# Edge softmax of a graph layer: whole-tile sums repaired at their first and last node, and x loads issued at its outset

## The reference

```python
w = exp(scores - smax[dst])                     # smax: largest score of the node's edges, per head
alpha = w / maximum(segment_sum(w, dst)[dst], 1e-9)
pooled[:, h] = segment_sum(alpha[:, h:h+1] * p, dst)
mean_p = segment_sum(p, dst) / maximum(deg, 1)
gate = softmax(mean_p @ Wg.T + bg)              # over the 4 heads
out = x + sigmoid(sum over h of gate[:, h] * pooled[:, h])
```

## Time and profile before

| what | us |
|---|---|
| median of 3 runs | 880.24 (876.46 to 882.37) |
| profiled execution, its own time | 881.09 |
| its span, first to last instruction | 879.3 |
| DVE busy in the span | 528.9 |
| PE busy in the span | 558.0 |
| HBM read and written | 111.39 MB and 59.59 MB |

### The profile page before, as it was taken

One profiled execution on the slowest core, in us unless ns is written; L12 is line 12 of the kernel. 1 busy time (PEld: TensorE's weight loads), 2 busy tenths in 40 slices (PEclk: granted clock), 3 DMA queues, 4 the chain that ended last, 5 costly groups with the idle time before them and its releaser, 6 DMA issues.

```text
span 879.3 us, 12486 instructions
## 1 busy us (share of the span) xinstructions
PE 558.0 (63%) x2436; PEld 425.6 (48%) x2437; DVE 528.9 (60%) x1878; ACT 378.0 (43%) x645; POOL 437.8 (50%) x334
## 2 busy tenths in 40 slices
PE   4104211117999999688950006988887888877885
PEld 3002101105877776566730005867776666656664
DVE  3621010015999999777988895756665555555553
ACT  0011000004777776455720020445665666576564
POOL 5777777730000004565200000557777778787887
PEclk9655555556999999999985556999999999999998
DMA  6334434311333434877600004999999999999998
GB/s 177 103 106 127 130 104 129 105 50 53 117 111 106 120 98 125 261 242 240 224 27 0 0 0 148 302 386 322 305 323 339 311 304 336 336 333 327 339 333 299
DMA packets 135059, 171.41 MB, mean 195 GB/s; under 512 B 8110, under 2 KB 121604, under 8 KB 135022
## 3 DMA queue, kind: packets, MB, share of 16 engines
q10 hardware_dynamic: 90496, 89.83, 31.3%
q1 hardware_dynamic: 31678, 42.99, 15.7%
q0 software_dynamic: 12848, 38.20, 13.9%
HBM read 111.39 MB, written 59.59 MB: 194 GB/s over the span
## 4 chain that ended last, share of the span: by engine, by line
PE 40%; another core or an unknown queue 19%; DVE 12%; issue 11%; ACT 7%; POOL 4%; ACTq 3%; DVEq 2%; DMA 2%; POOLq 0%
PE bank L555 19%; PE bank L613 14%; PE bank L545 6%; ACT arena L429 4%; POOL arena L327 3%; DVE spread L913 3%; ACT bank L402 2%; DMA arena<-in_x_dram 2%; DVE arena L867 2%; ACTq L432 1%; DVEq L917 1%; DVE arena L827 1%; DVE arena L822 1%; DVEq L913 1%
## 5 line engine op out<-in xcount | busy, mean ns | idle before, releaser
L327 POOL TENSOR_TENSOR arena<-arena 128x1024 f32<-128x1024 f32 x96 | 224.8, 2350 | 185.7 <-ACT arena L429 184.8
L613 PE MATMUL bank<-p_keep,spread 128*128 x1172 | 278.0, 392 | 57.9 <-DVE spread L913 47.8
L555 PE MATMUL bank<-w_all,arena 128*128 128x264 f32 (+1 forms) x784 | 226.7, 415 | 104.4 <-issue 81.3
L913 DVE TENSOR_SCALAR spread<-bank,rel,wgt 128x128 f32<-128x128 f32 x586 | 195.8, 404 | 136.5 <-PE bank L613 84.8
L613 PEld LDWEIGHTS bank<-p_keep,spread 128*128 128x128 f32 x1172 | 222.0, 194 | 113.7 <-issue 84.8
L555 PEld LDWEIGHTS bank<-w_all,arena 128*128 128x128 f32 (+1 forms) x784 | 143.5, 204 | 127.2 <-issue 86.3
L314 POOL DMA_INDIRECT arena<-in_x_dram,idx x72 | 69.3, 962 | 190.8 <-ACT arena L366 170.2
L429 ACT ACTIVATE arena<-bank 128x1024 f32<-128x1024 f32 x97 | 99.2, 1022 | 150.2 <-PE bank L613 133.7
L374 ACT ACTIVATE arena<-bank 128x256 f32<-128x256 f32 x196 | 72.6, 371 | 169.6 <-remote 108.6
L314 POOL DMA_INDIRECT p_keep<-in_x_dram,idx x124 | 118.4, 955 | 43.0 <-issue 37.5
L545 PE MATMUL bank<-ident,arena 128*128 128x128 f32 x392 | 83.5, 297 | 62.3 <-remote 46.7
(11 more groups left out here) (161 smaller groups left out, 184.5 us busy)
## 6 DMA issues: line engine op xcount, KB each, us to landing
out_dram<-arena ACTq DMA_DIRECT2D x97, 512.0 KB, 4.4
arena<-in_x_dram ACTq DMA_DIRECT2D x73, 512.0 KB, 5.3
arena<-in_edge_attr_dram SPq DMA_DIRECT2D x48, 512.0 KB
arena<-in_x_dram POOLq DMA_DIRECT2D x24, 512.0 KB, 5.7
p_spill<-p_keep SPq DMA_DIRECT2D x16, 512.0 KB
p_keep<-p_spill SPq DMA_DIRECT2D x16, 512.0 KB, 5.3
p_keep<-in_x_dram,idx POOLq DMA_INDIRECT x124
arena<-in_x_dram,idx POOLq DMA_INDIRECT x72
```

The source lines that it names most:

```text
L327: pool.tensor_tensor(yout[:, slot, :, :], yout[:, slot, :, :], xin[:, slot, :, :], ALU.add).then_inc(summed, 1)
L555: last = nc.tensor.matmul(bank[0:n, 2 + t % 4, 0:NT], msg_t[:, t % 4, c, 0:n], w_all[:, c, :], start=(c == 0), stop=(c == KD - 1))
L613: nc.tensor.matmul(places[:, bass.ds(place, T)], spread[:, k0 + k, :], p_rows[:, bass.ds(p_at, T)], start=False, stop=True, skip_group_che ...
L913: v.tensor_scalar(spread[:, k, :], bank[:, 7, P:2 * P], rel[:, bass.ds(s0 + k, 1)], wgt[:, bass.ds(s0 + k, 1)], ALU.is_equal, ALU.mult).th ...
```

## The change

In the softmax each tile's own maxima serve its exponentials, and its own sums serve all its edges. The first and the last node of every tile, which may go on elsewhere, get their own small computation on 128 x 2 x 2 values per row (`own`, `far`, `mine`, `gain`, `ex`, `mn`), and the edges of these two nodes get their `c` by two predicated copies at the end. The eight rows are read from PSUM by the scans directly. Whether a node goes on is read from `next_f`, which five loads of single elements fill in the prologue; the bias of the gate is added to the matmul's bias there. The x loads of the first four groups are issued after the last normalization. `c` is ordered in two parts, 128 columns first, and DVE's first turn of the pooling is written out so that the rest is copied after it.

The diff, with the declarations of tiles left out:

```diff
 @block.sync
-sp.wait_ge(pads_set, 2)
+sp.wait_ge(pads_set, 3)
...
+    ends_of = dst[0:(TILES - 1) * P].rearrange("(t e) -> t e", e=P)
+    sp.dma_start(next_i[1:P, 0, 0:1], ends_of[0:P - 1, P - 1:P]).then_inc(next_in, 16)
+    sp.dma_start(next_i[0:TILES - P, 1, 0:1], ends_of[P - 1:TILES - 1, P - 1:P]).then_inc(next_in, 16)
+    sp.dma_start(next_i[0:P, 0, 1:2], ends_of[1:P + 1, 0:1]).then_inc(next_in, 16)
+    sp.dma_start(next_i[0:TILES - 2 - P, 1, 1:2], ends_of[P + 1:TILES - 1, 0:1]).then_inc(next_in, 16)
+    last_tile = (TILES - 1) * P
+    sp.dma_start(next_i[TILES - 2 - P:TILES - 1 - P, 1, 1:2],
+                 dst[last_tile:last_tile + 1].rearrange("(t e) -> t e", e=1)).then_inc(next_in, 16)
...
+pool.memset(next_i[:, :, :], -1).then_inc(pads_set, 1)
...
+act.wait_ge(ln_done, TILES)
+for g in range(XS):
+    load_x(g, g)
+
+act.wait_ge(keep_turned, 1)
+turned_keep = bank[0:C, 5, :].rearrange("p (s t) -> p s t", s=2)
+nc.scalar.activation(keep_row, turned_keep, ACT.Copy).then_inc(keep_set, 1)
+nc.scalar.activation(keep_neg, turned_keep, ACT.Copy, scale=BIG, bias=-BIG).then_inc(keep_set, 1)
+
 act.wait_ge(diff_ready, 1)
-nc.scalar.activation(val[:, 0:H, :], val[:, 0:H, :], ACT.Exp).then_inc(exp_done, 1)
-
+nc.scalar.activation(w_run, w_run, ACT.Exp).then_inc(exp_done, 1)
 act.wait_ge(diff_ready, 2)
-nc.scalar.activation(run[:, H:K, :], run[:, H:K, :], ACT.Exp).then_inc(exp_done, 1)
-
-
+nc.scalar.activation(ex, ex, ACT.Exp).then_inc(exp_done, 1)
+act.wait_ge(diff_ready, 3)
+nc.scalar.activation(run[:, 0:H, :], run[:, 0:H, :], ACT.Exp).then_inc(exp_done, 1)
+act.wait_ge(diff_ready, 4)
+nc.scalar.activation(mn, mn, ACT.Exp).then_inc(exp_done, 1)
...
+act.wait_ge(rows_read, 1)
...
-for g in range(XS):
-    load_x(g, g)
...
+pe.wait_ge(keep_ready, 1)
+turn_ends(lambda b, side: keep_cols[:, b, side, :], C, 5).then_inc(keep_turned, 1)
+pe.wait_ge(ends_ready, 1)
+turn_ends(lambda b, side: top[:, :, edge_of(b, side)], H, 6).then_inc(ends_turned, 1)
+turn_chain(H, 1)
+pe.wait_ge(ends_ready, 2)
+turn_ends(lambda b, side: own[:, b, side, :], C, 6).then_inc(ends_turned, 1)
+turn_chain(C, 2)
 pe.wait_ge(c_ready, 1)
-by_step(lambda b: flag[:, 2, b * P:(b + 1) * P], sel_1, 6, wgt_summed)
+c_of = lambda b: run[:, 8, b * P:(b + 1) * P]
+for n, o, cols in ((7, 2 * P, slice(0, P)), (6, 0, slice(P, STEPS))):
+    for b in range(BLK):
+        last = nc.tensor.matmul(bank[:, n, o:o + cols.stop - cols.start], c_of(b), sel_1[:, b, cols],
+                                start=(b == 0), stop=(b == BLK - 1))
+    last.then_inc(wgt_summed, 1)
...
+then(v.tensor_copy(bias[:, T:NT], bank[:, 4, KD * K:(KD + 1) * K]))
+then(v.tensor_tensor(bias[:, T + H:NT], bias[:, T + H:NT], bg_b[:, :], ALU.add))
+dve.wait_ge(next_in, 80)
+v.tensor_copy(next_f[:, :, :], next_i[:, :, :])
...
+v.memset(joins[:, 0:RW + 1:P], 0.0)
+then(v.tensor_tensor(per_blk(same)[:, :, 1:P], dst_f[:, :, 1:P], dst_f[:, :, 0:P - 1], ALU.is_equal))
+v.memset(tot[:, 0, :], 1.0)
+v.tensor_scalar(neg, joins, 1.0, BIG, ALU.subtract, ALU.mult)
+v.tensor_tensor(cm, next_f[:, :, :], dst_f[:, :, 0:P:P - 1], ALU.is_equal)
+then(v.tensor_tensor(one_node, dst_f[:, :, 0], dst_f[:, :, P - 1], ALU.is_equal))
+then(v.tensor_tensor(wc, cm, for_b(one_node), ALU.mult))
+v.tensor_copy(keep_cols, for_k(wc, C)).then_inc(keep_ready, 1)
+dve.wait_ge(rows_turned, 1)
+for n in range(H):
+    ins = v.tensor_tensor_scan(w_run[:, n, :], neg_same, row(n), 0.0, ALU.add, ALU.max)
+then(ins)
+dve.wait_ge(rows_turned, 2)
+for n in range(H):
+    ins = v.tensor_tensor_scan(top[:, n, ::-1], neg_next[:, ::-1], w_run[:, n, ::-1], -BIG,
+                               ALU.add, ALU.max)
+then(ins)
+dve.sem_inc(ends_ready, 1)
+v.tensor_tensor(w_run, bank[:, 0:2, :].rearrange("p b (k e) -> p (b k) e", k=2), top, ALU.subtract
+                ).then_inc(diff_ready, 1)
+for n in range(H, K):
+    v.tensor_tensor_scan(run[:, n, :], same, row(n), 0.0, ALU.mult, ALU.add)
+v.tensor_tensor_scan(run[:, K, :], same, tot[:, 0, :], 0.0, ALU.mult, ALU.add).then_inc(rows_read, 1)
+v.tensor_scalar(cneg, cm, 1.0, BIG, ALU.subtract, ALU.mult)
+v.tensor_scalar(wneg, one_node, 1.0, BIG, ALU.subtract, ALU.mult)
 v.tensor_scalar(end, same_next, -1.0, 1.0, ALU.mult, ALU.add)
+def link(k, keeps, pad, ops, count):
+    dve.wait_ge(ends_turned, count)
+    ends = bank[0:k, 6, :].rearrange("p (s t) -> p s t", s=2)
+    v.memset(chain_pads, pad)
+    v.tensor_tensor_scan(chain[0:k, 0, 1:TP + 1], keeps[0:k, 0, :], ends[:, 1, :], pad, *ops)
+    then(v.tensor_tensor_scan(chain[0:k, 1, 0:TP][:, ::-1], keeps[0:k, 1, ::-1], ends[:, 0, ::-1], pad, *ops))
+    dve.sem_inc(chain_ready, 1)
+from_far = bank[:, 7, 2 * P:2 * P + BLK * 2 * C].rearrange("p (b s k) -> p b s k", b=BLK, s=2)
+dve.wait_ge(keep_set, 2)
+link(H, keep_neg, -BIG, (ALU.add, ALU.max), 1)
+dve.wait_ge(exp_done, 1)
+for n in range(H):
+    ins = v.tensor_tensor_scan(run[:, n, :], same, w_run[:, n, :], 0.0, ALU.mult, ALU.add)
+then(ins)
+then(v.tensor_tensor(run, run, end.unsqueeze(1).broadcast_to([P, C, RW]), ALU.mult))
+dve.wait_ge(chain_turned, 1)
+own_top = at_ends(top, H)
+then(v.tensor_tensor(far_m, from_far[:, :, :, 0:H], for_k(cneg, H), ALU.add))
+v.tensor_tensor(m_all, own_top, far_m, ALU.max)
+then(v.tensor_tensor(ex, swap(far_m), for_k(for_b(wneg), H), ALU.add))
+then(v.tensor_tensor(m_all, m_all, ex, ALU.max))
+v.tensor_tensor(ex, own_top, m_all, ALU.subtract).then_inc(diff_ready, 1)
+for n in range(C):
+    ins = v.tensor_tensor_scan(tot[:, n, ::-1], same_next[:, ::-1], run[:, n, ::-1], 0.0,
+                               ALU.mult, ALU.add)
+then(ins)
+dve.wait_ge(exp_done, 2)
+own_tot = at_ends(tot, C)
+v.tensor_tensor(own[:, :, :, 0:H], own_tot[:, :, :, 0:H], ex, ALU.mult)
+then(v.tensor_copy(own[:, :, :, H:C], own_tot[:, :, :, H:C]))
+dve.sem_inc(ends_ready, 1)
+over_h = lambda a: a.unsqueeze(1).broadcast_to([P, H, RW])
+deg = run[:, 8, :]
+then(v.tensor_scalar(deg, tot[:, K, :], 1.0, None, ALU.max))
+then(v.reciprocal(deg, deg))
+then(v.tensor_tensor(run[:, 0:H, :], tot[:, H:K, :], over_h(deg), ALU.mult))
+link(C, keep_row, 0.0, (ALU.mult, ALU.add), 2)
+then(v.tensor_tensor(run[:, 4:6, :], run[:, 0:2, :], run[:, 2:4, :], ALU.max))
+then(v.tensor_tensor(run[:, 4, :], run[:, 4, :], run[:, 5, :], ALU.max))
+v.tensor_tensor(run[:, 0:H, :], run[:, 0:H, :], over_h(run[:, 4, :]), ALU.subtract).then_inc(diff_ready, 1)
+dve.wait_ge(chain_turned, 2)
+flat3 = lambda a: a.rearrange("p b s k -> p (b s) k")
+flat2 = lambda a: a.rearrange("p b s -> p (b s)")
+mine = own
+then(v.tensor_tensor(far, from_far, for_k(cm, C), ALU.mult))
+v.tensor_tensor(mine, mine, far, ALU.add)
+then(v.tensor_tensor(far_w, swap(far), for_k(for_b(one_node), C), ALU.mult))
+then(v.tensor_tensor(mine, mine, far_w, ALU.add))
+then(v.tensor_scalar(dg, mine[:, :, :, K], 1.0, None, ALU.max))
+then(v.reciprocal(flat2(dg), flat2(dg)))
+then(v.tensor_tensor(mn, mine[:, :, :, H:K], for_k(dg, H), ALU.mult))
+then(v.tensor_reduce(flat2(mx), flat3(mn), AX.X, ALU.max))
+v.tensor_tensor(mn, mn, for_k(mx, H), ALU.subtract).then_inc(diff_ready, 1)
+sums, total = tot[:, 0:H, :], run[:, 8, :]
+pair = lambda a: a.rearrange("p (g k) e -> p g k e", g=2)
+then(v.tensor_scalar(sums, sums, 1e-9, None, ALU.max))
+then(v.tensor_tensor(tot[:, 4:6, :], pair(sums)[:, :, 0, :], pair(sums)[:, :, 1, :], ALU.mult))
+v.tensor_tensor(tot[:, 6, :], tot[:, 4, :], tot[:, 5, :], ALU.mult)
 for b in range(BLK):
+    v.tensor_scalar(sel_1[:, b, :], step_tile[:, :], tile_f[:, b:b + 1], None, ALU.is_equal)
+dve.wait_ge(exp_done, 3)
+eg = run[:, 0:H, :]
+v.tensor_tensor(run[:, 4:8, :], w_run, eg, ALU.mult)
+then(v.tensor_tensor(tot[:, 7:9, :], run[:, 0:2, :], run[:, 2:4, :], ALU.add))
+v.tensor_tensor(tot[:, 7, :], tot[:, 7, :], tot[:, 8, :], ALU.add)
+then(v.tensor_tensor(pair(run[:, 4:8, :]), pair(run[:, 4:8, :]), pair(sums)[:, :, ::-1, :], ALU.mult))
+dve.wait_ge(exp_done, 4)
+then(v.tensor_reduce(flat2(se), flat3(mn), AX.X, ALU.add))
+then(v.tensor_scalar(far[:, :, :, 0:H], mine[:, :, :, 0:H], 1e-9, None, ALU.max))
+then(v.tensor_tensor(far_m, far[:, :, :, 0:H], for_k(se, H), ALU.mult))
+v.reciprocal(far_m.rearrange("p b s k -> p (b s k)"), far_m.rearrange("p b s k -> p (b s k)"))
+then(v.tensor_tensor(m_all, mn, ex, ALU.mult))
+v.tensor_tensor(gain, m_all, far_m, ALU.mult)
+then(v.tensor_tensor(tot[:, 6, :], tot[:, 6, :], tot[:, 7, :], ALU.mult))
+v.reciprocal(tot[:, 6, :], tot[:, 6, :])
+then(v.tensor_tensor(run[:, 0:2, :], pair(run[:, 4:8, :])[:, :, 0, :], pair(run[:, 4:8, :])[:, :, 1, :], ALU.add))
+then(v.tensor_tensor(run[:, 2:4, :], run[:, 0:2, :], tot[:, 5:3:-1, :], ALU.mult))
+v.tensor_tensor(total, run[:, 2, :], run[:, 3, :], ALU.add)
+by_end = lambda b, side: run[:, 4 + side, b * P:(b + 1) * P]
+for h in range(H):
+    for b in range(BLK):
+        for side in range(2):
+            w_of, g_of = w_run[:, h, b * P:(b + 1) * P], gain[:, b, side, h:h + 1]
+            if h == 0:
```

(67 more changed lines are left out.)

166 lines of the change are left out of this document (42 added, 124 removed).

## The result

The changed kernel takes 844.41 us (median, 843.76 to 848.87), the kernel before 878.35 us (876.19 to 882.37) in runs beside it: a ratio of 0.9619, 95% interval 0.9567 to 0.9671, 33.9 us less. Forecast were 850.0 us and 30.2 us less. The profiled execution took 844.58 us, with a span of 842.8. All ratios here leave out the executions in which the chip was in a slower state; the medians do not.

The account below looks back on a forecast made before the run. DVE was taken to bound the softmax, and bytes most of the pooling. From the profiled 881.09 us, - 28.5 - 2.0 + 0.3 = 850.9, or 850.0 against the median 880.24; range 842 to 857.

Parts of the forecast that it names:

- DVE bounds the softmax, and what it is spared comes off in full: Softmax start to `c_ready`, 81.4 us: DVE is busy for 74.2, so whatever it is spared the whole kernel is spared.
- The new sequence, 52.9 us: Softmax on DVE, priced instruction by instruction up to `c_ready`: 52.9 us against 81.4, a gain of 28.5 us.
- Nothing late in the hand-offs' place: Softmax: work between each question and its answer removes 5 us of DVE waiting; a failed cover would cost about 1 us.
- From `c_ready` to the first step, 6.3 us: Ordering before the pooling: 6.3 us instead of 8.3, a gain of 2.0 us, bounds 0.8 and 3.5.
- The x loads are worth nothing: Four loads of 512 KB moved from the pooling's start into the softmax: none credited, bounds 0 and 6.3 us.
- The prologue, 0.3 us: Five single-element loads ahead of the weights on SP, plus POOL's memset, cost 0.3 us in all, bounds 0 and 1.5.
- The x loads (1): Rival, chance 0.12: the moved x loads' 6.3 us come off the pooling's saturated stretch, giving 843.7 us.
- a dear sequence (3): Rival, chance 0.12: softmax small operations at 0.3 us each, dear predicated copies and one cover gone add 7.3 us: 857.
- The clock (2): Rival, chance 0.10: at the pooling's start TensorE's clock returns sooner, saving 2.0 us, giving 848.0.
- (4): Rival, chance 0.02: slower, since PE's clock stays at 0.50 at the pooling's start; 75 us of it would give 884.
- (5): Rival, chance 0.02: the main loop lands elsewhere, a few slow tiles more or less, 3 to 5 us either way.
- The prediction's last sign of being wrong: Pooling, first matmul to the end: the forecast is wrong if it takes 334 or 346 us, not 340 as now.

Follow-up runs that it names:

- The test without the merge: Kernel before without the merge of the carries into every edge (52 SCALAR_TENSOR_TENSORs and two masks): 692.26 us against 705.39, ratio 0.981.
- The kernel with one copy: Changed kernel, but DVE waits for both parts of the ordering before it copies `wgt`: 848.42 us, ratio 0.9716 to the kernel before.
- the last four runs: Changed kernel 677.04 us; with single-element loads behind the weights 668.08; that plus 32 PE transposes 671.58; kernel before with those loads ahead of the weights 712.38.

## Why the prediction was right, point by point

**DVE bounds the softmax, and what it is spared comes off in full: right.** The test without the merge gave 14.8 us for 14.7 in the stretch. In the whole time it gave 13.1 us, with an interval of 10 to 17, so that some of it could be lost behind.

**The new sequence, 52.9 us: measured 50.3.** The dear terms were sized well: scans 17.9 for 18.3, the 1024s 6.0 for 6.2, the twelve SCALAR_TENSOR_TENSORs 3.5 for 3.5, the two predicated copies 0.46 each for 0.45. What was too dear was the small change: 31 small operations took 4.6 us for 5.6, since many have no wait behind them, and the next instruction starts some 0.1 us after them; and the hand-offs 0.14 where they occur at all, some 0.6 for 1.2. The scans that read PSUM took 0.60 us each, like the others, so reading PSUM directly was free and the four copies were saved. The Trainium skill, "VectorE: DVE Perf Modes", section "Rules for kernel authors", says to copy PSUM to SBUF first where many operations follow; for these scans the trace shows nothing that the copy would have gained.

**Nothing late in the hand-offs' place: right.** DVE has no wait above 0.15 us between 452.45 and 502.7.

**From `c_ready` to the first step, 6.3 us: measured 4.1.** What failed here is the step by which DVE's spreads could start only behind PE's other 458 columns. DVE in order of time, changed kernel:

```profile
504.06 0.29 DVE L997 COPY wgt<-bank 128x128 f32<-128x128 f32 x1 [1.37 <-PE bank L666]
505.68 3.92 DVE L1003 TENSOR_SCALAR spread<-bank,rel,wgt 128x128 f32<-128x128 f32 x12 [1.32 <-issue]
509.51 0.63 DVE L1015 COPY wgt<-bank 128x458 f32<-128x458 f32 x1
```

The spreads start at 505.68 us, while PE's ordering runs to 507.08. So PE had added to `stepped` before its matmuls were through, which the prediction gave as a bound only (3.5 us of gain). The three spreads hide too, and the gain is 4.1, outside the bounds.

**The x loads are worth nothing: right,** within the 1 to 2 us that putting them back can tell. But the DMA share at the outset was to fall by 0.3 and fell by 0.18 (0.14 between the two profiles on one chip). The rates say how much of the room was left free: with the x loads gone it is 257 - 211 = 46 GB/s less over 22 us, 1.0 of the 2.1 MB, though PE also did more steps (99 records against 91); in the two profiles on one chip, with PE's steps alike (99 and 98), it is 286 - 219 = 67 GB/s, 1.5 MB. So some 0.6 MB of other transfers did come forward into the room, against the prediction's reasoning, and still no time came of it that can be told.

**The prologue, 0.3 us: wrong in size where it counts.** SP's queue, changed kernel:

```profile
4.61 0.25 SPq L271 DMA_DIRECT2D next_i<-in_dst_dram  x1
4.90 2.48 SPq L272 DMA_DIRECT2D next_i<-in_dst_dram  x1
7.42 0.35 SPq L273 DMA_DIRECT2D next_i<-in_dst_dram  x1
...
8.53 0.43 SPq L278 DMA_DIRECT2D p_keep<-in_L_gnn_W_fc_dram  x1
```

One of the five issues took 2.48 us, all 3.9, where five at 0.45 would be 2.3. (POOL's memset did no harm: the first gather came at 8.78 us, not 9.0.) That the gathers hide the tables' lateness was true of the chip whose profile was at hand, and there even 39 us of it (first statistics at 75.2 and not 35.9) could not be told from drift. On the other kind it is false: 4.6 us.

**The rivals.** The x loads (1) and a dear sequence (3) fell. The clock (2) came in, with a chance of 0.10: the granted clock in the first pooling steps was 0.50 for 1.1 to 1.5 us instead of 4.4, and the first sigmoid came 10.9 us behind the first matmul instead of 12.5, 1.6 of the rival's 2.0 us. The kernel with one copy shows that it is the split, which takes away PE's idle time, that does it. The forecast had this at nothing. (4) did not occur. (5), drift of the main loop's end, is real: 447.4 to 452.5 us in six profiles on the first kind of chip. The prediction's last sign of being wrong, a pooling of 334 or 346 us instead of 340, could not serve: 335.9 us were measured, and in fourteen profiles the pooling took 333.0 to 342.0, with either softmax.

**The total, partly by luck.** In the two measurements on the first kind of chip it was 33.9 and 29.9 us, on the second kind 29.9, for a forecast of 30.2. By the profiles' stretches it should be 31.2 + 4.1 + 1.2 to 1.5 = 36.5 to 36.8 us, less the loads' 0 or 4.6 us. So the terms were forecast some 6 us too small (2.6 in the softmax, 2.1 ahead of the first step, 1.5 of the clock), and the totals came near for other reasons. On the second kind the loads' price makes up most of it: 32 us expected, 29.9 measured. On the first kind nothing that was found does. In the first measurement nearly 3 us are missing, in the second nearly 7, which is more than its interval allows (28 to 33 us saved). The kernel before has no profile from that chip, so where they went, into a later end of the main loop or a longer pooling, is open.

**What is best.** The changed kernel with its five loads behind the weights: 668.1 us against 677.0 and 706.9 on one chip, and 841.2 against 843.5 and 873.5 on another, where the gain over the changed kernel isn't shown.

## What to carry to other kernels

A stretch that is one engine's sequence can be priced instruction by instruction from the profile; count the start-to-start time, and for small ones whether a wait follows. Before crediting a transfer that is moved, look whether its engines have room where it is now. A few tiny loads ahead of something that all wait for can cost more than the clever part around them saves, and one profile may hide it: run on a second chip.

## What the runs showed of the hardware that was not expected

**Two kinds of chip.** While POOL issues its gathers, the hand-offs between the other engines crawl on some chips and not on others. Windows of the changed kernel, columns as in the earlier trace rows, first on the chip of the first result, then on that of the last four runs:

```profile
100.00:200.00 100.00, 24.05 (x60) 14.41 (x60) 11.24 (x45) 9.08 (x22) 64.54 (x68) 0.52 0.37 106
```

```profile
100.00:200.00 100.00, 99.87 (x500) 72.51 (x498) 99.32 (x458) 71.75 (x189) 72.25 (x75) 1.00 0.68 207
```

PE starts 60 matmuls in 100 us on the one and 500 on the other. From 200 to 300 us, when POOL issues no gather, the first profile has 468. The gathers that come later, from 350 to 400 us, slow it far less: 177 in 50 us. On the first chip, DVE goes on 22 us after PE's work for it is done:

```profile
21.61 3.29 PE L588 MATMUL bank<-p_keep,ones 128*128 128x512 f32 x8
...
46.99 0.29 DVE L747 COPY bank<-p_keep 128x128 f32<-128x128 f32 x1 [26.12 <-remote]
```

In all executions of a chip it was the one or the other: the kernel before took 871 to 877 us in eleven runs on one, 702 to 713 in 34 runs on two others. What makes the difference was not tried, and stays open.

**POOL and DVE at once.** Two instructions of 586 columns on POOL made three DVE instructions beside them 0.3 to 0.5 us longer each; work moved to an idle POOL was paid for on DVE.
